# Causal clearing moved from GpSimd to VectorE, and longer lots of probability sums, in an attention-plus-experts kernel on one core

## The chip, the cores and the metric

The kernel runs on one core of a Trainium2 chip. The metric is the device time in microseconds (us) of the whole program. The kernel before took 1740.67 us, the median of 3 runs (1737.72 to 1743.27).

## The reference

What is computed, cut down (x is 2 x 2048 x 512, 16 heads of 32):

```
xn = layernorm(x)
q, k, v = split(xn @ W_qkv)                        # 16 heads of 32
a = q @ k.T / sqrt(32) + alibi + causal_mask       # 2048 x 2048 per head
y = softmax(a) @ v @ W_o
e = argmax(softmax(xn @ wg));  f = gate * (xn @ W[e].T + b[e])   # top-1 of 8 experts
out = x + y + f
```

## The kernel before

The program has four stages: projection and routing, attention (`attend`), the experts, and the sum of the parts. The change touches `attend`, and one line of set-up in the first stage.

**Tiling.** `attend` handles 8 groups of 4 heads (`G`, `HG`). Scores are held transposed, keys on the 128 partitions and queries along the row. A group has 40 rounds (`ROUNDS`): for query chunk c = 0 to 3 (512 queries each) the key blocks 0 to 4c+3 of 128 keys. Chunk 0 is rounds 0 to 3, chunk 1 rounds 4 to 11, chunk 2 rounds 12 to 23, chunk 3 rounds 24 to 39. The last four rounds of each chunk cross the diagonal (`DIAG_OF`, 16 in a group); there only the columns from `off` on are computed, and the 128 x 128 square at `off` has an upper triangle that must be zero.

**A round.** TensorE makes 4 score tiles (L1208, into 3 PSUM banks in turn), ScalarE takes their exponential into `probs` (L1136; 4 slots, so that round r reuses the slot of round r - 4), and later TensorE multiplies the values by it (L1252, `y_ps`). The sums of the softmax (`den_ps`) come from a product with ones. For diagonal rounds it is made from `probs` itself (L1243). The other rounds are first added up on GpSimd in lots (`QUAD_ROUNDS`): `add_quad` makes 4 additions of 128 x 512 for the first two rounds of a lot (L985) and 4 for each further round (L992), and TensorE makes one product for the whole lot (`quad_product`, L1215), two rounds after its last round. Two `quad_sum` buffers are used in turn.

**Waits around the lots.** ScalarE may not write round r before GpSimd has added round r - 4 (`added`, `added_by`): the first two rounds of a lot are released together by its first 4 additions, each further round by its own 4.

**Clearing.** On GpSimd, `clear` zeroes the triangle in all 4 heads of a diagonal round with one instruction (L1001), which signals `cleared`; TensorE waits for it before it uses that round. GpSimd's queue is in order of `SUMMED_OR_CLEARED`: each lot at its last round, each clear at its round, and four multiplications a group (`normalise`, L975).

**VectorE** computes ahead the maximum of each row of scores: TensorE makes `max_ps` tiles (L1176, 3 banks in turn, so that it makes the fourth only when VectorE has taken the first), and VectorE takes the maximum (L1038, and L1034 on the diagonal). A group needs 160 such units. `PLAN_MID` spreads them at 4 a round, rounds 14 on for the next group. In the last group only rounds 0 to 13 have any. VectorE also turns and inverts the sums of a finished chunk (`invert`, L1073, L1077, L1081), for chunk c at rounds 2, 3 and 4 after its last; these come after the maxima of their round.

**TensorE's order** is written out: it visits rounds in pairs. A visit to rounds r, r+1 has 8 score tiles with 8 maxima tiles between them (`visit`); after it come the row sums and value products of the pair before (r-2, r-1). Pairs are called by their rounds below.

**DMA.** The next group's `q_aug` and `k_aug` are loaded when the previous group has ended, and are needed at round 14.

## Time and profile before

| | |
|---|---|
| median of 3 runs | 1740.67 us |
| the profiled execution, whole time | 1743.71 us |
| its span in the profile | 1741.2 us |
| TensorE busy | 1627.1 us, 93% |
| VectorE busy | 1044.1 us, 60% |
| ScalarE busy | 749.0 us, 43% |
| GpSimd busy | 873.1 us, 50% |
| mean granted TensorE clock | 0.965 of full speed |

PE is TensorE, PEld its weight loads, DVE is VectorE, ACT ScalarE, POOL GpSimd. The span is that of the one profiled execution. Attention fills the stretch from 355 to 1470 us of it; its eight groups begin near 368, 550, 680, 812, 946, 1078, 1209 and 1341 us. A line in the timeline merges equal instructions that follow one another: start, time that they take together, engine, source line, operation, tiles, count, and in brackets the idle time of the engine before them with what ended it.

### The profile page before, as it was taken

What the parts mean: (1) busy time and instruction counts of PE and PEld (TensorE: products, weight loads), DVE (VectorE), ACT (ScalarE), POOL (GpSimd) and SP (SyncE); (2) the same over time, 40 slices, a digit from 0 to 9 for tenths busy, and PEclk for the clock granted to TensorE, in tenths of its full rate; (3) what the DMA queues carried; (4) which work ended last, traced back from release to release, by engine and by line L of the source; (5) the groups of instructions that cost most, each with busy time, mean ns of one, the idle gap of its engine ahead of it and who ended that gap; (6) DMA issues with size and microseconds to landing.
All of it is one profiled execution on the core that took longest, in us unless ns stands there. A gap on an engine that the chain in (4) does not pass through costs nothing. (4 is left out here: it accounts for less than half of the span.)

```text
span 1741.2 us, 26967 instructions
## 1 busy us (share of the span) xinstructions
PE 1627.1 (93%) x9266; PEld 991.7 (57%) x9267; DVE 1044.1 (60%) x2451; ACT 749.0 (43%) x1574; POOL 873.1 (50%) x869
## 2 busy tenths in 40 slices
PE   5999999589699999999999999999999997799898
PEld 4888888444344554545554554554545433588686
DVE  6443333488477776867776777777777601544466
ACT  3222222024354654655564655655555564411110
POOL 5500000017685874874875775775775775222350
PEclk9999999769899999999999999999999998899999
DMA  6655654685803603703702702802801401445695
GB/s 239 222 190 181 215 189 168 152 119 104 119 8 75 124 9 79 125 8 73 132 8 61 143 8 51 153 8 49 156 8 60 154 7 59 136 157 164 205 396 213
DMA packets 99244, 205.68 MB, mean 118 GB/s; under 512 B 11164, under 2 KB 28604, under 8 KB 93484
## 3 DMA queue, kind: packets, MB, share of 16 engines
q1 hardware_dynamic: 85208, 172.26, 39.0%
q0 software_dynamic: 9248, 23.53, 4.3%
q10 hardware_dynamic: 4672, 8.41, 1.7%
q8 instruction: 66, 1.08, 0.3%
q14 instruction: 50, 0.41, 0.1%
HBM read 124.55 MB, written 79.07 MB: 117 GB/s over the span
## 5 line engine op out<-in xcount | busy, mean ns | idle before, releaser
L1136 ACT ACTIVATE probs_sb<-score_ps 128x512 f32<-128x512 f32 (+3 forms) x1280 | 585.3, 552 | 475.3 <-PE score_ps L1208 454.9
L1038 DVE TENSOR_REDUCE part_max<-max_ps 128x1 f32<-128x512 f32 x768 | 473.0, 678 | 213.4 <-PE max_ps L1176 213.2
L1176 PE MATMUL max_ps<-k_aug,q_aug 104*128 104x512 f32 (+3 forms) x1280 | 509.2, 410 | 52.2 <-DMA k_aug<-steps_d 34.6
L1208 PE MATMUL score_ps<-q_aug,k_aug 106*128 106x512 f32 (+4 forms) x1280 | 480.1, 398 | 9.6 <-ACT probs_sb L1136 7.4
L985 POOL TENSOR_TENSOR quad_sum<-probs_sb 128x512 f32<-128x512 f32 x288 | 359.9, 1283 | 167.4 <-ACT probs_sb L1136 143.8
L1176 PEld LDWEIGHTS max_ps<-k_aug,q_aug 104*128 104x128 f32 x1280 | 247.7, 194 | 238.1 <-DVE part_max L1038 86.6
L1208 PEld LDWEIGHTS score_ps<-q_aug,k_aug 106*128 106x128 f32 (+1 forms) x1280 | 241.9, 190 | 145.8 <-ACT probs_sb L1136 122.5
L1252 PE MATMUL acc_ps<-probs_sb,v_sb 128*32 128x512 f32 (+3 forms) x2560 | 291.8, 542 | 0.0
L1034 DVE CUSTOM_DVE_ANT_0 max_ps<-max_ps,mask_row 128x384 f32<-128x384 f32 (+3 forms) x512 | 239.1, 513 | 68.9 <-PE max_ps L1176 67.8
L992 POOL TENSOR_TENSOR quad_sum<-quad_sum,probs_sb 128x512 f32<-128x512 f32 x192 | 239.2, 1284 | 0.1
L1001 POOL TENSOR_SCALAR_AFFINE_SELECT probs_sb<-probs_sb 128x512 f32<-128x512 f32 x128 | 80.3, 636 | 205.2 <-ACT probs_sb L1136 204.6
L1252 PEld LDWEIGHTS acc_ps<-probs_sb,v_sb 128*32 128x32 f32 x2560 | 73.5, 111 | 122.7 <-issue 89.6
L959 POOL IOTA token<- 128x32 int32 x1 | 0.2, 154 | 246.7 <-POOLq L393 246.7
L680 DVE SCALAR_TENSOR_TENSOR st_lo<-group_ps,st_hi 128x512 fp32r<-128x512 f32 x64 | 44.2, 691 | 127.2 <-ACT st_hi L732 127.2
L796 PE MATMUL group_ps<-xT_hi,w_hi 128*128 128x512 f32 x256 | 102.3, 399 | 0.0
L796 PE MATMUL group_ps<-xT_hi,w_lo 128*128 128x512 f32 x256 | 101.0, 395 | 0.0
L796 PE MATMUL group_ps<-xT_lo,w_hi 128*128 128x512 f32 x256 | 101.0, 394 | 0.0
L1243 PE MATMUL acc_ps<-probs_sb,ones 128*32 128x512 f32 (+3 forms) x1024 | 96.8, 450 | 0.0
L732 ACT ACTIVATE st_hi<-group_ps 128x512 fp32r<-128x512 f32 x64 | 38.3, 598 | 135.4 <-PE group_ps L796 135.4
L1353 POOL DMA_INDIRECT rows<-xn_d,slot_token x39 | 37.3, 958 | 99.5 <-PE turn_ps L1450 92.1
L1215 PE MATMUL acc_ps<-quad_sum,ones 128*32 128x512 f32 x576 | 75.8, 598 | 0.0
L1073 DVE STREAM_TRANSPOSE acc_sb<-acc_ps 128x512 f32<-128x512 f32 x32 | 22.9, 715 | 86.3 <-PE acc_ps L1252 84.9
(177 smaller groups left out, 1754.0 us busy)
## 6 DMA issues: line engine op xcount, KB each, us to landing
k_aug<-k_hi_d SPq DMA_DIRECT2D x14, 1024.0 KB
q_aug<-q_hi_d SPq DMA_DIRECT2D x14, 1024.0 KB
slot_y_d<-y_rows SPq DMA_DIRECT2D x39, 256.0 KB, 2.0
xn_d<-xn SPq DMA_DIRECT2D x8, 1024.0 KB, 5.5
q_hi_d<-st_hi SPq DMA_DIRECT2D x32, 256.0 KB, 3.5
q_lo_d<-st_lo SPq DMA_DIRECT2D x32, 256.0 KB, 3.6
k_hi_d<-st_hi SPq DMA_DIRECT2D x32, 256.0 KB, 2.5
k_lo_d<-st_lo SPq DMA_DIRECT2D x32, 256.0 KB, 2.8
```

What stands on the lines that cost most here:

```text
L796: last = nc.tensor.matmul(group_ps[:, n % BANKS], lhs, rhs, start=(k == 0 and p == 0), stop=(k == KC - 1 and p == 2))
L985: nc.gpsimd.tensor_tensor(quad_sum[:, t % 2, hh], probs[:, r0 % P_SLOTS, hh], probs[:, r1 % P_SLOTS, hh], ALU.add).then_inc(added, 1)
L992: nc.gpsimd.tensor_tensor(quad_sum[:, t % 2, hh], quad_sum[:, t % 2, hh], probs[:, r % P_SLOTS, hh], ALU.add).then_inc(added, 1)
L1001: nc.gpsimd.affine_select(out=square, in_=square, compare_op=ALU.is_ge, fill=0.0, base=0, pattern=[[0, HG], [1, P]], channel_multiplier=-1 ...
L1034: nc.vector.tensor_tensor_reduce(max_ps[:, bank, 0:w], max_ps[:, bank, 0:w], m.mask_row[:, CH - w:CH], 1.0, LOWEST, ALU.add, ALU.max, part ...
L1038: nc.vector.tensor_reduce(part_max[:, hh * QT + i, kc:kc + 1], max_ps[:, bank, 0:w], AX.X, ALU.max).then_inc(max_taken, 1)
L1136: nc.scalar.activation(probs[:, r % P_SLOTS, hh, off:CH], score_ps[:, (r * HG + hh) % S_BANKS, off:CH], ACT.Exp).then_inc(exp_done, 1)
L1176: nc.tensor.matmul(max_ps[:, bank, 0:w], q_aug[0:ROW_MAX, half, hh, i * P:(i + 1) * P], k_aug[0:ROW_MAX, half, hh, kc * CH:kc * CH + w], s ...
L1208: nc.tensor.matmul(score_ps[:, u % S_BANKS, off:CH], k_aug[rows, half, hh, jb * P:(jb + 1) * P], q_aug[rows, half, hh, cc * CH + off:(cc + ...
L1215: last = nc.tensor.matmul(den_ps[hh * DH:(hh + 1) * DH, :], m.ones[:], quad_sum[:, t % 2, hh], start=start, stop=False)
L1243: nc.tensor.matmul(den_ps[hh * DH:(hh + 1) * DH, off:CH], m.ones[:], probs[:, r % P_SLOTS, hh, off:CH], start=r == FIRST_SUM[cc], stop=r = ...
L1252: last = nc.tensor.matmul(y_ps[hh * DH:(hh + 1) * DH, off:CH], v_sb[:, half, jb, hh * DH:(hh + 1) * DH], probs[:, r % P_SLOTS, hh, off:CH] ...
```

## The change

Four things change.

1. The lots of chunk 2 become 4 and 4 rounds (4, 2, 2 before), those of chunk 3 become 4, 4, 2 and 2 (4, 2, 2, 2, 2 before). A group has 7 lots (9 before). GpSimd's additions go from 60 to 68 a group.
2. GpSimd no longer clears.
3. VectorE clears: after the maxima of the second round of a diagonal pair it waits for the exponentials of each round of the pair and takes the minimum of the square (128 x 512 over 4 heads, in place) and `keep`. In its queue this stands before `invert`.
4. A tile `keep` (128 x 128, bf16) of limits is made by GpSimd at the very start: 3e38 where the probability stays, 0 where it is to be cleared.

```diff
-LOT_SIZES = {1: (4,), 2: (4, 2, 2), 3: (4, 2, 2, 2, 2)}
+LOT_SIZES = {1: (4,), 2: (4, 4), 3: (4, 4, 2, 2)}
...
+        m.keep = sb("keep", [P, P], BF16)
...
-                for t in (m.ident, m.mask_row):
-                    nc.gpsimd.memset(t[:], 0.0).then_inc(blank, 1)
-                pool.wait_ge(blank, 2)
+                for t, fill in ((m.ident, 0.0), (m.mask_row, 0.0), (m.keep, -LOWEST)):
+                    nc.gpsimd.memset(t[:], fill).then_inc(blank, 1)
+                pool.wait_ge(blank, 3)
+                nc.gpsimd.affine_select(out=m.keep[:], in_=m.keep[:], compare_op=ALU.is_ge, fill=0.0, base=0,
+                                        pattern=[[1, P]], channel_multiplier=-1)
...
-                def clear(r, exps):
-
-                    cc, jb = ROUNDS[r]
-                    off = (jb - TPC * cc) * P
-                    square = probs[:, r % P_SLOTS, :, off:off + P]
-                    pool.wait_ge(exp_done, exps + (r + 1) * HG)
-                    nc.gpsimd.affine_select(out=square, in_=square, compare_op=ALU.is_ge, fill=0.0, base=0,
-                                            pattern=[[0, HG], [1, P]], channel_multiplier=-1).then_inc(cleared, 1)
...
-                        if r in DIAG_OF:
-                            clear(r, exps)
-                        else:
+                        if r not in DIAG_OF:
                             add_quad(QUAD_OF[r], first, exps, used, adds)
...
+                def clear(g, r):
+
+                    cc, jb = ROUNDS[r]
+                    off = (jb - TPC * cc) * P
+                    square = probs[:, r % P_SLOTS, :, off:off + P]
+                    dve.wait_ge(exp_done, g * NSU + (r + 1) * HG)
+                    nc.vector.tensor_tensor(square, square, m.keep[:].unsqueeze(1).to_broadcast([P, HG, P]),
+                                            ALU.min).then_inc(cleared, 1)
...
                     for r in range(NR):
                         maxima(events[r], banks, g, units)
+                        if r % 2 and r in DIAG_OF:
+                            clear(g, r - 1)
+                            clear(g, r)
                         if r in INVERT_AT:
```

## Rows read from the trace of the kernel before

**Rows 1.** Third and last group: length, busy of each engine, PEclk, DMA share, GB/s

```profile
680.00:812.00 132.00, 130.43 (x844) 66.83 (x844) 95.95 (x244) 74.86 (x168) 89.56 (x80) 0.99 0.37 70
1341.00:1468.00 127.00, 119.56 (x749) 52.01 (x737) 38.30 (x87) 74.01 (x166) 89.28 (x80) 0.97 0.21 75
```

**Rows 2.** Groups of instructions by form: busy, mean ns | idle before, releaser

```profile
L985 POOL TENSOR_TENSOR quad_sum<-probs_sb 128x512 f32<-128x512 f32 x210 | 262.6, 1284 | 126.3 <-ACT probs_sb L1136 107.0 <-PE acc_ps L1215 19.3
L1001 POOL TENSOR_SCALAR_AFFINE_SELECT probs_sb<-probs_sb 128x512 f32<-128x512 f32 x93 | 58.3, 636 | 116.3 <-ACT probs_sb L1136 115.9
L1551 DVE TENSOR_TENSOR yT_lo<-yT,yT_hi 128x2048 fp32r<-128x2048 f32 x8 | 18.2, 2290 | 21.0 <-ACT yT_hi L1545 21.0
L627 DVE TENSOR_TENSOR more_than<-run,full_f 128x256 f32<-128x256 f32 x1 | 0.4, 427 | 0.0
```

**Rows 3.** Timeline of TensorE, chunk 2 of the third group

```profile
753.35 1.06 PE L1243 MATMUL acc_ps<-probs_sb,ones 128*32 128x512 f32 x8
...
755.10 1.04 PE L1215 MATMUL acc_ps<-quad_sum,ones 128*32 128x512 f32 x8
755.95 0.83 PE L1243 MATMUL acc_ps<-probs_sb,ones 128*32 128x384 f32 x8
```

**Rows 4.** Timelines of VectorE and TensorE, chunk 0 of the fourth group

```profile
816.34 0.71 DVE L1073 STREAM_TRANSPOSE acc_sb<-acc_ps 128x512 f32<-128x512 f32 x1
816.97 2.45 DVE L1038 TENSOR_REDUCE part_max<-max_ps 128x1 f32<-128x512 f32 x4
...
820.18 0.50 PE L1176 MATMUL max_ps<-k_aug,q_aug 104*128 104x512 f32 x1
820.61 1.06 PE L1243 MATMUL acc_ps<-probs_sb,ones 128*32 128x512 f32 x8
```

**Rows 5.** Timeline of VectorE, pairs that follow (8, 9) and (20, 21)

```profile
749.91 2.48 DVE L1038 TENSOR_REDUCE part_max<-max_ps 128x1 f32<-128x512 f32 x4 [2.54 <-PE max_ps L1176]
...
841.83 4.87 DVE L1038 TENSOR_REDUCE part_max<-max_ps 128x1 f32<-128x512 f32 x8 [1.27 <-PE max_ps L1176]
```

**Rows 6.** Timeline of GpSimd, additions of chunks 2, 3 and 1

```profile
738.43 9.94 POOL L985 TENSOR_TENSOR quad_sum<-probs_sb 128x512 f32<-128x512 f32 x8
...
777.04 9.99 POOL L985 TENSOR_TENSOR quad_sum<-probs_sb 128x512 f32<-128x512 f32 x8
...
832.27 9.98 POOL L992 TENSOR_TENSOR quad_sum<-quad_sum,probs_sb 128x512 f32<-128x512 f32 x8
```

**Rows 7.** Timeline of ScalarE: exponentials of pairs (22, 23), (34, 35), (36, 37), (0, 1)

```profile
750.11 1.51 ACT L1136 ACTIVATE probs_sb<-score_ps 128x256 f32<-128x256 f32 x5 [2.85 <-PE score_ps L1208]
...
789.76 4.03 ACT L1136 ACTIVATE probs_sb<-score_ps 128x512 f32<-128x512 f32 x8 [2.76 <-PE score_ps L1208]
796.62 3.60 ACT L1136 ACTIVATE probs_sb<-score_ps 128x512 f32<-128x512 f32 x8 [2.83 <-PE score_ps L1208]
...
813.07 3.60 ACT L1136 ACTIVATE probs_sb<-score_ps 128x512 f32<-128x512 f32 x8 [6.13 <-PE score_ps L1208]
```

**Rows 8.** The last group: additions, and exponentials of pairs (22, 23) and (36, 37)

```profile
1397.91 5.01 POOL L985 TENSOR_TENSOR quad_sum<-probs_sb 128x512 f32<-128x512 f32 x4
1435.62 9.90 POOL L985 TENSOR_TENSOR quad_sum<-probs_sb 128x512 f32<-128x512 f32 x8
1410.49 2.13 ACT L1136 ACTIVATE probs_sb<-score_ps 128x256 f32<-128x256 f32 x8 [2.49 <-PE score_ps L1208]
1454.51 3.60 ACT L1136 ACTIVATE probs_sb<-score_ps 128x512 f32<-128x512 f32 x8 [2.34 <-POOL quad_sum L985]
```

**Rows 9.** TensorE's waits for the next group's load; VectorE in the first group

```profile
PE max_ps L1176 <- DMA q_aug<-q_rows_d: 3.1, 3, 1.5
468.55 0.30 DVE L1034 CUSTOM_DVE_ANT_0 max_ps<-max_ps,mask_row 128x128 f32<-128x128 f32 x1 [14.34 <-PE max_ps L1176]
```

**Rows 10.** Start of two groups, third and fourth: the granted clock (PEclk)

```profile
689.00:693.00 4.00, 4.00 (x32) 0.94 (x24) 1.28 (x3) 0.00 (x0) 1.27 (x1) 0.71 1.02 203
820.00:824.00 4.00, 3.85 (x35) 1.37 (x35) 2.53 (x5) 0.28 (x1) 1.91 (x2) 1.00 1.04 207
```

## Prediction

> **What bounds the kernel now.** First the busy time by stretch. In a middle group of 132 us TensorE is busy for 130.4, VectorE for 96.0, GpSimd for 89.6 [rows 1]: TensorE's written order sets the pace, and what lengthens or shortens one of its steps moves the end. But a matmul that waits for its data counts as near-full too, so I read the timelines to see who releases the next step. Three helpers come close. VectorE paces the maxima tiles: in the last visit of chunk 0 TensorE makes its eighth maxima tile at 820.18, when VectorE has just taken the fifth (it takes one each 0.61, from 816.97, with a short reciprocal after four), and only then starts the row sums at 820.61 [rows 4]. GpSimd paces the reuse of `probs`: additions follow one another every 1.24 to 1.25 us (9.94 / 8) [rows 6]. And the next group's load ends last in three of the middle groups, 3.1 us in all [rows 9]. Group totals hide all three, so the sum has to be made place by place.
>
> **What is saved.** A lot's product holds TensorE from 755.10 to the next product at 755.95, 0.85 us [rows 3]. Two lots fewer in a group, one after visit (20, 21) and one after visit (32, 33), are 1.7 us a group, 13.6 in eight. GpSimd loses 16 clears of 0.636 a group (10.2 us) and gains 8 additions of 1.284 (10.3 us) [rows 2]: its total stays, but the additions come in the two chunks where they are dense and the clears went from places where it idled.
>
> **What a clear costs on VectorE.** No row shows this minimum. The two rows with both inputs in SBUF take 427 ns for 256 columns and 2290 for 2048 [rows 2]: 1.04 ns a column, so 0.69 us for 512 columns, and a pair of clears holds the engine for 1.3 (queued instructions overlap by some 0.07, as the maxima do: 4.87 / 8 = 0.61 [rows 5]). Beside an addition of GpSimd its price is unknown: the rows show none of VectorE's two-input instructions there. Below, it is 0.69 as alone; above, the two take turns, and each clear may wait for a whole addition of 1.28 and hold up the next by 0.65. I take turns as the likelier. GpSimd's addition with two inputs takes twice its select with one (1.284, 0.636 [rows 2]), so fetching the inputs is what it spends its time on, and an engine's second input is just what is new here on VectorE. That is thin evidence, so both sums are given.
>
> The Trainium skill says it outright (SBUF — State Buffer, "Who interferes with whom"): VectorE and GpSimd share a pair of ports as an exclusive lock, and a VectorE instruction with two SBUF inputs contends with a GpSimd instruction that reads SBUF. No row here shows it; by it the upper sum holds, without it the lower.
>
> **Chunk 0, pair (0, 1).** The clears wait for the exponentials, done at 813.07 + 3.60 = 816.67 [rows 7]. Queued behind them are the transpose of the sums, begun at 816.34, and the maxima of the next visit, begun at 816.97 [rows 4]. New first take: 816.67 + 1.3 + 0.63 = 818.6, 1.6 us late. There is no idle time to hide it: visits (0, 1) and (2, 3) follow each other with no products between, and by rows 4 the row sums start with VectorE's fifth take. **+1.6.** The clears of (2, 3) fall in the products after it, and GpSimd is idle at both.
>
> **Chunk 1, pair (8, 9).** VectorE idles 1.27 before 841.83 [rows 5], so it is free at 840.56, and 1.3 just fits: **0** alone. But GpSimd adds until 832.27 + 9.98 = 842.25 [rows 6], with a boundary at 841.0. In turns the first clear runs from 841.0 to 841.7, the second straight after it or after the last addition, and the first take comes at 842.4 or 843.7, 0.6 or 1.8 late: **+1.2**. TensorE's maxima pass it on.
>
> **Chunk 2.** Before, the additions of 16 to 19 ran as eight from 738.43 [rows 6]. Now they are twelve: 738.43 + 12 x 1.245 = 753.4. The exponential of round 23 may not begin before that. It began at 750.11 + 4 x 0.31 = 751.35 [rows 7] and could now begin at 750.5 with the product gone. TensorE's last score tile of the visit needs that exponential's bank, so it follows at 753.7, a maxima tile after it, and the row sums start at 754.4 instead of 753.35 [rows 3]: **+1.05**, the saved 0.85 already counted. In turns, the clears of (20, 21), asked for at 749.91 - 2.54 = 747.4 [rows 5], fall among these additions and push the twelfth to 754.7: **+2.35**. The clears of (22, 23) are hidden in the products that follow.
>
> **Chunk 3.** Here the first twelve additions are as before; from 777.04 come twelve (eight before) [rows 6], done at 792.0. The exponential of round 35 began at 789.76 + 4 x 0.5 = 791.8 [rows 7]: +0.2, again with the 0.85 eaten. The next four additions end at 797.0, and round 36, begun at 796.62 [rows 7], waits for them: **+0.4**, with turns at (36, 37) **+0.6**.
>
> **Middle groups:** alone 1.6 + 0 + 1.05 + 0.4 = 3.05, in turns 1.6 + 1.2 + 2.35 + 0.6 = 5.75. Six of them: 18.3 or 34.5. The load waits swallow up to 3.1 of it [rows 9], since the load begins with the group and is needed at round 14: 15.2 or 31.4.
>
> **Last group.** No maxima after round 13, VectorE almost idle (38.3 us [rows 1]), but the rounds are faster, so GpSimd is closer to the bound. 1.6 and 0 or 1.2 as above; chunk 2: 1397.91 + 12 x 1.245 = 1412.85, in turns 1414.15, against 1410.49 + 1.3 = 1411.8 for round 23: +1.05 or +2.35; chunk 3: 1435.62 + 16 x 1.245 = 1455.5 against 1454.51 for round 36 [rows 8]: +1.0, with turns 1.1. Together 3.65 or 6.25.
>
> **First group.** Chunk 2 ends in a 14.3 us wait for the next load [rows 9], which hides it. Left are +1.6 in chunk 0, 0 or 1.2 in chunk 1, and -0.85 in chunk 3, where its rounds are slower: 0.75 or 2. The tile `keep` costs GpSimd some half microsecond at the start, behind the first loads: 0.
>
> **Sum:** alone 15.2 + 3.65 + 0.75 = +19.6; in turns 31.4 + 6.25 + 2 = +39.6. On the profiled execution's 1743.7 (1741.2 span and 2.5 around it) that is 1763.3 and 1783.3. It lay 3.0 above the median of 1740.7, so in terms of the median 1760 and **1780**. I forecast 1780.
>
> **Rivals.** (a) *Clears run free beside additions:* the alone sum, 1760. For it: nothing in the rows shows turns. Against: the argument above. (b) *Everything is hidden, the products go:* 1740.7 - 13.6 = 1727. It needs the twelve additions of chunk 2 to end by 750.5 instead of 753.4, and a free 1.3 us on VectorE at 816.7. It decides from a pitch of addition below (750.5 - 738.43) / 12 = 1.0 us, which no row shows, unless ScalarE's wait is looser than I read it. Half of the gain, with losses of the same size, would be no change. (c) *The clock drops more often:* at the end of chunk 0 the third group ran at a mean of 0.71 for 4 us where the fourth ran at 1.00 [rows 10], so partly at 1.2 GHz and not 2.4, and the fifth did as the third, just after the visit whose TensorE work was stretched by VectorE. Those two groups lost about 1.6 us there. With that visit stretched further, it may come in all eight: six more times some 1.4 is +8, 1788.
>
> **How the numbers follow.** In turns 0.50, rival (a) and what lies between 0.28, (c) 0.10, (b) 0.08, no change 0.04. The range is 1752 to 1797: below, the alone sum with half of its chunk 0 cost hidden; above, (c) with second clears that always wait. Within 0.3% (5 us) is what a measurement can't tell from no change. Faster 0.08, same 0.04, slower 0.88.
>
> **What would show it.** VectorE's first take after (0, 1) some 2 us behind the last exponential; ScalarE's idle time before round 23 put down to GpSimd's additions; additions in an unbroken row of twelve; in turns, gaps or longer records of both engines around 841 and 748; 448 products L1215 instead of 576; the group's period grown from 132 to about 138 us (135 alone). Wrong would be: a VectorE minimum much shorter than 0.69, additions that run faster in long rows, or a group's period below 131.

## The result, and the profile after

The changed kernel takes **1831.12 us** (median of 4 runs, 1825.09 to 1831.95), the kernel before on the same chip 1739.20 (4 runs, 1736.08 to 1743.27): a ratio of 1.052, 95% interval 1.050 to 1.055. The forecast was 1780 in a range of 1752 to 1797. The sign was right; the loss is 92 us where 39 were forecast.

The groups of instructions of the changed kernel first, by line and form (busy, mean ns of one, idle before).

```profile
L1082 DVE TENSOR_TENSOR probs_sb<-probs_sb,keep 128x512 f32<-128x512 f32 x128 | 146.8, 1186 | 55.7 <-ACT probs_sb L1140 55.7
L995 POOL TENSOR_TENSOR quad_sum<-quad_sum,probs_sb 128x512 f32<-128x512 f32 x320 | 398.4, 1285 | 0.0
L1219 PE MATMUL acc_ps<-quad_sum,ones 128*32 128x512 f32 x448 | 61.8, 626 | 0.0
```

L1219 is the lots' product (576 before, now 448: the change does that part). GpSimd's additions have kept their 1.28. The clear, L1082, has a mean of 1.19. Asked for by its line, it shows what a mean hides:

```profile
L1082 DVE TENSOR_TENSOR probs_sb<-probs_sb,keep x128: 668/682/7154, 377.5 to 1552.5; 128x512 f32<-128x512 f32 x128
```

The median is 0.68, just what was worked out for it (0.69), and the longest 7.15 (in the last group, where VectorE had been idle before it). In the first group no pair takes over 1.4; from the second on some wait, and in the middle groups it is the same three in each. The timeline of VectorE and GpSimd in the third group at these pairs, (8, 9), (20, 21) and (36, 37):

```profile
724.87 4.20 DVE L1082 TENSOR_TENSOR probs_sb<-probs_sb,keep 128x512 f32<-128x512 f32 x2
...
719.20 7.49 POOL L995 TENSOR_TENSOR quad_sum<-quad_sum,probs_sb 128x512 f32<-128x512 f32 x6
726.64 1.28 POOL L978 TENSOR_TENSOR acc_sb<-acc_sb 128x512 f32<-128x512 f32 x1
...
766.17 7.12 DVE L1082 TENSOR_TENSOR probs_sb<-probs_sb,keep 128x512 f32<-128x512 f32 x2
...
762.24 9.90 POOL L995 TENSOR_TENSOR quad_sum<-quad_sum,probs_sb 128x512 f32<-128x512 f32 x8
...
826.01 1.46 DVE L1082 TENSOR_TENSOR probs_sb<-probs_sb,keep 128x512 f32<-128x512 f32 x2
```

Read the ends. The additions of chunk 2 end at 762.24 + 9.90 = 772.14, and the two clears at 773.29, 1.15 later: the first was asked for 0.2 into an addition (762.24 + 3 x 1.24 = 765.96) and has waited for the rest of it and for four more. At (8, 9) GpSimd is done at 727.92 (additions and a multiplication, back to back), and the pair at 729.07, again 1.15 later. At (36, 37) little was left to wait for: that run ended 0.3 after the pair asked. So VectorE did not take turns with GpSimd: it waited for the end of the unbroken run, and GpSimd wasn't slowed at all (8 additions in 9.90, as [rows 6]). Before, VectorE had 2.54 of idle time after (20, 21) and 1.27 after (8, 9) [rows 5]; 7.12 and 4.20 don't fit in. TensorE, and the windows around it, in the same place:

```profile
773.95 0.79 PE L1180 MATMUL max_ps<-k_aug,q_aug 104*128 104x512 f32 x1 [4.92 <-DVE part_max L1030]
```

```profile
769.00:771.00 2.00, 0.02 (x1) 0.00 (x0) 2.00 (x1) 0.48 (x2) 2.00 (x3) 1.00 0.01 4
771.00:773.00 2.00, 0.00 (x0) 0.00 (x0) 2.00 (x2) 0.00 (x0) 1.14 (x1) 0.74 0.00 0
773.00:777.00 4.00, 3.05 (x13) 2.44 (x17) 4.00 (x10) 1.11 (x4) 0.00 (x0) 0.50 0.01 4
```

(The columns are those of [rows 1].) TensorE stands still for 4.92 because VectorE, which holds its three maxima banks, stands in the clear. Then it pays a second time: from 773 to 777 the granted clock is 0.50, that is 1.2 GHz and not 2.4. The forecast expected something else here, a wait of ScalarE for the additions before round 23. In the middle groups there is none: those exponentials wait for TensorE, which has stopped for VectorE (timeline of ScalarE, third group). Only in the last group does ScalarE wait there for the additions, 2.32.

```profile
774.97 0.28 ACT L1140 ACTIVATE probs_sb<-score_ps 128x128 f32<-128x128 f32 x1 [5.48 <-PE score_ps L1212]
```

The list of waits says the same of the whole program. Before, the first of these waits wasn't in it, and the longest of the second was 0.8 us:

```profile
PE max_ps L1180 <- DVE part_max L1030: 57.9, 39, 5.0
PEld max_ps L1180 <- DVE part_max L1030: 132.8, 211, 5.2
```

**Where the 88 us of span went.** A chunk's length is the time between ScalarE's copies of a finished chunk out of PSUM (L1115 before, L1119 after), read from ScalarE's timeline. In the fourth group of after the copies give 16.1, 31.2 and 45.0 for chunks 0, 1 and 2 (the copy at 841.24 is that of the third group's last chunk):

```profile
841.24 0.69 ACT L1119 ACTIVATE acc_sb<-acc_ps 128x512 f32<-128x512 f32 x1
857.37 0.60 ACT L1119 ACTIVATE acc_sb<-acc_ps 128x512 f32<-128x512 f32 x1 [0.71 <-PE acc_ps L1256]
888.56 0.60 ACT L1119 ACTIVATE acc_sb<-acc_ps 128x512 f32<-128x512 f32 x1 [0.89 <-PE acc_ps L1256]
933.54 0.60 ACT L1119 ACTIVATE acc_sb<-acc_ps 128x512 f32<-128x512 f32 x1 [0.89 <-PE acc_ps L1256]
```

The table sums these lengths over the second to the eighth group, each less the same of before, in us. The column for the first group runs from its first copy to its fourth, so its chunk 0 isn't in it. All versions of the attention kernel in the next section are in the table. Two things in it aren't the work of the edits. The kernel before waits for the next group's load ahead of round 14 in three groups, which makes its chunk 1 about 3.7 longer in all; a version without these waits shows -3.7 there. And its chunk 0 ran at a lower clock in two groups.

| kernel | chunk 0 | chunk 1 | chunk 2 | chunk 3 | first group | sum |
|---|---|---|---|---|---|---|
| forecast, in turns | +11.2 | +8.4 | +16.5 | +4.7 | +2.0 | +42.8, less 3.1 of load waits |
| after | +18.5 | +28.6 | +37.5 | +4.2 | -0.4 | +88.4 |
| a_lots: the lots alone | +4.8 | -1.7 | +16.9 | +3.1 | -0.2 | +22.9 |
| b_clears: the clears alone | +18.5 | +28.5 | -2.0 | -1.2 | +0.8 | +44.6 |
| c_oneinput | +19.0 | -3.7 | +16.2 | +4.2 | -0.4 | +35.3 |
| d_hand | +19.6 | -1.9 | +30.8 | +4.7 | +1.6 | +54.7 |
| f_zero | +1.7 | -1.2 | +30.9 | +4.7 | +1.7 | +37.7 |
| i_step | +17.3 | +17.7 | +55.4 | +41.3 | +1.5 | +133.2 |
| g_4242 | -1.7 | -1.4 | -1.0 | -3.6 | -0.7 | -8.4 |

### The profile page after: what moved, and what is told of

It is laid out like the page before. It is cut to its first block and busy times, and to the rows that moved or that the text cites. A ratio compares the mean times of both kernels' runs of the same rounds, so it can differ in the third digit from the quotient of the medians.

```text
span 1829.1 us, 26873 instructions
## 1 busy us (share of the span) xinstructions
PE 1653.8 (90%) x9138; PEld 1005.8 (55%) x9139; DVE 1181.6 (65%) x2579; ACT 750.5 (41%) x1574; POOL 872.3 (48%) x807
## 5 line engine op out<-in xcount | busy, mean ns | idle before, releaser
L1180 PE MATMUL max_ps<-k_aug,q_aug 104*128 104x512 f32 (+3 forms) x1280 | 524.7, 427 | 103.4 <-DVE part_max L1030 57.9
L988 POOL TENSOR_TENSOR quad_sum<-probs_sb 128x512 f32<-128x512 f32 x224 | 279.8, 1286 | 311.2 <-ACT probs_sb L1140 311.2
L1180 PEld LDWEIGHTS max_ps<-k_aug,q_aug 104*128 104x128 f32 x1280 | 257.2, 201 | 284.1 <-DVE part_max L1030 132.8
L995 POOL TENSOR_TENSOR quad_sum<-quad_sum,probs_sb 128x512 f32<-128x512 f32 x320 | 398.4, 1285 | 0.0
L1212 PEld LDWEIGHTS score_ps<-q_aug,k_aug 106*128 106x128 f32 (+1 forms) x1280 | 250.6, 197 | 156.7 <-ACT probs_sb L1140 133.7
L1256 PE MATMUL acc_ps<-probs_sb,v_sb 128*32 128x512 f32 (+3 forms) x2560 | 298.2, 558 | 0.0
L1082 DVE TENSOR_TENSOR probs_sb<-probs_sb,keep 128x512 f32<-128x512 f32 x128 | 146.8, 1186 | 55.7 <-ACT probs_sb L1140 55.7
L978 POOL TENSOR_TENSOR acc_sb<-acc_sb 128x512 f32<-128x512 f32 x32 | 41.1, 1284 | 167.4 <-DVE acc_sb L1073 167.3
L1247 PE MATMUL acc_ps<-probs_sb,ones 128*32 128x512 f32 (+3 forms) x1024 | 112.2, 515 | 0.0
L1026 DVE DVE_READ_ACCUMULATOR2_ANT part_max<- 128x1 f32 x512 | 72.2, 141 | 0.0
```

The lines of the kernel that those rows point to most:

```text
L988: nc.gpsimd.tensor_tensor(quad_sum[:, t % 2, hh], probs[:, r0 % P_SLOTS, hh], probs[:, r1 % P_SLOTS, hh], ALU.add).then_inc(added, 1)
L995: nc.gpsimd.tensor_tensor(quad_sum[:, t % 2, hh], quad_sum[:, t % 2, hh], probs[:, r % P_SLOTS, hh], ALU.add).then_inc(added, 1)
L1026: nc.vector.tensor_tensor_reduce(max_ps[:, bank, 0:w], max_ps[:, bank, 0:w], m.mask_row[:, CH - w:CH], 1.0, LOWEST, ALU.add, ALU.max, part ...
L1082: nc.vector.tensor_tensor(square, square, m.keep[:].unsqueeze(1).to_broadcast([P, HG, P]), ALU.min).then_inc(cleared, 1)
L1180: nc.tensor.matmul(max_ps[:, bank, 0:w], q_aug[0:ROW_MAX, half, hh, i * P:(i + 1) * P], k_aug[0:ROW_MAX, half, hh, kc * CH:kc * CH + w], s ...
L1212: nc.tensor.matmul(score_ps[:, u % S_BANKS, off:CH], k_aug[rows, half, hh, jb * P:(jb + 1) * P], q_aug[rows, half, hh, cc * CH + off:(cc + ...
```

## The experiments

The theories: **RUN** (a clear on VectorE waits for the end of GpSimd's unbroken run, that is of additions that follow one another without a gap), **TURNS** (it waits for one addition at most, as forecast), and the granted clock as a second payer. Diffs are against the changed kernel where nothing else is said.

### One half of the change at a time, and the clear without its second input

a_lots has the new lots and the clears of before on GpSimd; b_clears the clears on VectorE and the old lots:

```diff
-LOT_SIZES = {1: (4,), 2: (4, 4), 3: (4, 4, 2, 2)}
+LOT_SIZES = {1: (4,), 2: (4, 2, 2), 3: (4, 2, 2, 2, 2)}
```

c_oneinput keeps every wait and puts an instruction with one SBUF input in the clear's place. It leaves the clearing out (the triangles stay as they are).

```diff
-                    nc.vector.tensor_tensor(square, square, m.keep[:].unsqueeze(1).to_broadcast([P, HG, P]),
-                                            ALU.min).then_inc(cleared, 1)
+                    nc.vector.tensor_reduce(square, square.unsqueeze(3), AX.X, ALU.max).then_inc(cleared, 1)
```

> The longer lots alone, GpSimd still clears. Three theories of the changed kernel's +92 us. RUN: a VectorE instruction with two SBUF inputs waits until GpSimd's unbroken run of instructions ends, however long. TURNS: it waits for the one addition in flight, as the prediction had it. LOTS: the longer lots themselves cost most of it, through ScalarE's wait for the additions. RUN and TURNS expect what the prediction worked out for additions that come late less the saved products: +1.05 and +0.4 in a middle group, some 2 in the last, -0.85 in the first, so about +10, 1749 to 1750 us. LOTS expects 1790 or more.

> The clears on VectorE alone, the old lots. RUN: in chunk 1 the run of 12 additions is the same, so the pair (8, 9) still costs some 3.8 us a group; in chunk 2 the additions end at about the time the clears are asked for, so the 5.6 us there go nearly all; chunk 0 keeps 3.4. Eight times some 7.5 is +55 to +60, 1795 us, and no clear record over some 5 us. TURNS: 1.6 and 1.2 a group and the clock, under +30, 1765. LOTS: within 10 us of before.

> The changed kernel with a VectorE instruction of one SBUF input (a maximum over an axis of length one, in place, 128 x 512) in the place of each minimum; same place, same waits, about the same length. It leaves out the clearing of the triangles. RUN and TURNS: every record is 0.68 us whatever GpSimd does; chunk 1 costs nothing, chunk 2 about 1, chunk 0 keeps 3.4, so about +36 to +40, 1775 us. If the wait has nothing to do with the second input (a queue, the exponentials, the place in the order), the time stays at 1831 and records of 4 and 7 us remain.

Measured, beside 1741.63 of before (7 runs) on the same chip: a_lots **1766.82** (ratio 1.015, 1.011 to 1.018), b_clears **1785.47** (1.025, 1.023 to 1.027), c_oneinput **1778.88** (1.021, 1.019 to 1.023).

c_oneinput by the clear's line:

```profile
L1082 DVE TENSOR_REDUCE probs_sb<-probs_sb x128: 662/679/689, 375.7 to 1498.1; 128x512 f32<-128x512 f32 x128
```

The longest of 128 is 0.689, though it falls beside the same additions. With one input nothing waits: chunk 1 is back at its old length (25.8 us in every group, 30.4 on the mean with the minimum), and 1.3 us of VectorE cost nothing there. So the two-input minimum is what waits, and the whole price of that is 88.4 - 35.3 = 53 us of the 88. The masked maxima of the changed kernel have two inputs as well, but one of them in PSUM (`max_ps`). 362 of the 512 begin beside one of GpSimd's additions, and the longest of those takes 0.737, where one without an addition beside it has taken 0.735 (by the line of the masked maxima, in ns):

```profile
L1026 DVE CUSTOM_DVE_ANT_0 max_ps<-max_ps,mask_row x512: 275/502/737, 342.7 to 1467.9; 128x128 f32<-128x128 f32 x43, 128x384 f32<-128x384 f32 x43, 128x512 f32<-128x512 f32 x43, 128x256 f32<-128x256 f32 x42
```

So it is the second input in SBUF that matters, and not two inputs as such. In chunk 1 the wait delays VectorE by 4.20 - 1.27 = 2.9 a group and TensorE stops for 2.4. That makes 25.8 + 2.9 = 28.7; what the groups take is 29.6 or 31.2, at a lower clock (windows that each hold exactly chunk 1, third and fourth group of after):

```profile
713.79:743.37 29.58, 27.08 (x169) 13.99 (x170) 25.90 (x47) 14.65 (x33) 16.35 (x14) 0.94 0.88 153
857.37:888.56 31.19, 28.70 (x169) 14.38 (x170) 25.90 (x47) 14.63 (x33) 16.35 (x14) 0.89 0.84 147
```

So the wait for the run is behind all of the loss in chunk 1, and 0.9 to 2.5 us of it a group is the clock (an estimate, from these lengths).

b_clears shows the same with the old lots. Its 1785 lies between the 1795 that RUN expected and the 1765 of TURNS; what tells them apart is chunk 1, +28.5, the same as in the changed kernel and more than three times what turns were forecast to cost. Its pair (20, 21) waits too, 2.23 us, to the end of the run (753.64 + 9.94 = 763.58) and 1.16 on:

```profile
762.51 2.23 DVE L1082 TENSOR_TENSOR probs_sb<-probs_sb,keep 128x512 f32<-128x512 f32 x2
...
753.64 9.94 POOL L988 TENSOR_TENSOR quad_sum<-probs_sb 128x512 f32<-128x512 f32 x8
```

That wait costs nothing in chunk 2, since the run ends early enough. In chunk 2 the halves don't add: -2.0 and +16.9 apart, +37.5 together. The missing 22.6 come with the clears of (20, 21), which meet a run with four more additions to come only where the lot is four rounds long (with the old lots only its end, above). The second input alone, after less c_oneinput, is 37.5 - 16.2 = 21.3.

a_lots: the forecast for this half was 1.05 us for chunk 2 of each group; it is 16.9 / 7 = 2.4. ScalarE's wait is where it was forecast, at the exponential of round 23 (fourth group; timeline of ScalarE and GpSimd, and the windows after it):

```profile
887.76 0.62 ACT L1136 ACTIVATE probs_sb<-score_ps 128x128 f32<-128x128 f32 x3 [2.79 <-POOL quad_sum L992]
...
877.75 9.93 POOL L992 TENSOR_TENSOR quad_sum<-quad_sum,probs_sb 128x512 f32<-128x512 f32 x8
```

```profile
886.00:888.00 2.00, 0.44 (x1) 0.19 (x1) 1.53 (x6) 0.24 (x2) 2.00 (x3) 0.80 0.00 0
888.00:894.00 6.00, 5.91 (x26) 1.69 (x30) 0.63 (x2) 0.65 (x4) 2.03 (x4) 0.50 0.00 0
894.00:896.00 2.00, 2.00 (x22) 0.85 (x15) 0.03 (x1) 0.00 (x0) 0.00 (x0) 0.99 0.00 0
```

TensorE idles 1.6 us in 886 to 888, and for the 6 us behind it the clock is at 1.2 GHz. The idle is what the sum counted; the slow stretch is what it left out. c_oneinput shows the two apart, since its stop of 1.6 comes in every middle group but the clock doesn't fall in two of them (windows that each hold exactly chunk 2, fourth and third group):

```profile
869.58:909.04 39.46, 37.55 (x243) 19.59 (x244) 29.50 (x91) 22.55 (x51) 31.03 (x26) 1.00 0.03 11
732.13:774.72 42.59, 40.66 (x243) 20.21 (x244) 29.52 (x91) 22.56 (x51) 31.05 (x26) 0.92 0.03 8
```

Before it was 38.62: +0.84 at full clock, near the forecast 1.05, and 3.1 more at 0.92. (a_lots' third group, 37.90, has no stop at all in chunk 2; it had waited 1.57 for its load just ahead of it.)

### The clock in chunk 0

Chunk 0 has no additions beside it, and the one-input clear costs it as much as the minimum (+19.0, +18.5), so no second input is at work there. Windows that each hold exactly chunk 0: of before, the second and the third group; of after, the second and the third; of c_oneinput, the fourth.

```profile
553.63:566.48 12.85, 12.28 (x96) 6.52 (x95) 10.11 (x25) 6.96 (x19) 5.21 (x6) 1.00 1.03 204
684.23:698.67 14.44, 13.88 (x96) 6.82 (x95) 10.10 (x24) 6.96 (x18) 5.21 (x6) 0.88 1.02 203
```

```profile
554.64:568.69 14.05, 12.50 (x96) 6.51 (x95) 12.52 (x29) 6.96 (x19) 3.33 (x3) 1.00 1.02 202
697.48:713.79 16.31, 15.01 (x96) 7.59 (x95) 12.52 (x28) 6.95 (x19) 3.31 (x3) 0.79 1.02 203
```

```profile
828.46:843.76 15.30, 13.89 (x95) 6.93 (x95) 12.47 (x27) 6.95 (x18) 3.31 (x3) 0.89 1.02 203
```

The same 96 matmuls take 12.85, 14.05, 14.44, 15.30 or 16.31 us. At a clock of 1.00 the clears cost 14.05 - 12.85 = 1.2, the delay of VectorE itself (forecast 1.6). The rest is the clock: 0.88 or 0.89 costs 1.3 to 1.6 (15.30 - 14.05, 14.44 - 12.85), and 0.79 costs 2.3 (16.31 - 14.05). Before, two groups of seven were at 0.88; after, six of seven are at 0.79. Ahead of the fall in the third group stands a stop of TensorE for want of a maxima bank (1.01 us, then the clock row of the next 5 us). The same stop stands in the second group, at 557.05, and there the clock stays at 1.00:

```profile
557.05 0.50 PE L1180 MATMUL max_ps<-k_aug,q_aug 104*128 104x512 f32 x1 [1.01 <-DVE part_max L1030]
699.88 0.50 PE L1180 MATMUL max_ps<-k_aug,q_aug 104*128 104x512 f32 x1 [1.01 <-DVE part_max L1030]
```

```profile
699.00:700.00 1.00, 0.12 (x1) 0.12 (x2) 1.00 (x3) 0.30 (x1) 0.00 (x0) 1.00 0.96 188
700.00:705.00 5.00, 4.99 (x21) 2.63 (x25) 5.00 (x10) 1.11 (x4) 0.00 (x0) 0.53 1.04 206
```

Nor does the fall need this stop. In a_lots, where chunk 0 is as before and GpSimd clears, five of seven groups are at 0.88 (before: two), with no stop of TensorE over 0.32 us there; that is its +4.8. Its fourth group:

```profile
818.62:833.07 14.45, 13.91 (x96) 6.83 (x95) 10.11 (x25) 6.97 (x19) 5.21 (x6) 0.88 1.03 204
```

Counted over all versions, chunk 0 was below full clock in 11 of 28 groups where GpSimd clears it (before, a_lots, f_zero, g_4242), never below 0.88, and in 34 of 35 where VectorE does (after, b_clears, c_oneinput, d_hand, i_step), 21 of them at 0.79 or 0.80. So the clears there make the fall nearly certain and often deeper; what decides in the single group stays open.

This is rival (c) of the prediction, which had a chance of 0.10 and was priced at 1.4 for six groups; here it is paid in chunk 0 and again in chunks 1 and 2.

### GpSimd hands over

If GpSimd stops for the clears at a chosen place, the wait for the run should go. d_hand makes it wait for the pair (8, 9) before the last addition of round 7, and for (20, 21) before the first of round 19. f_zero has this and the clears of chunk 0 back on GpSimd, with a semaphore of their own (`cleared0`).

```diff
+                HANDOVER = {(7, HG - 1): 9, (19, 0): 21}
...
+                            if (r, hh) in HANDOVER:
+                                pool.wait_ge(cleared, clears + (DIAG_OF[HANDOVER[r, hh]] + 1))
```

```diff
+                        if r < TPC:
+                            clear_first(r, exps)
+                        elif r not in DIAG_OF:
...
-                        if r % 2 and r in DIAG_OF:
+                        if r % 2 and r in DIAG_OF and r >= TPC:
```

> The changed kernel with two gaps made in GpSimd's runs: before the last addition of round 7 it waits for the clears of (8, 9), before the first addition of round 19 for those of (20, 21). RUN: VectorE gets in at once; chunk 1 falls from +3.8 to about +1, chunk 2 from +5.6 to about +2.4, six us a group less, 1783 us, although GpSimd now waits more. TURNS: VectorE would have got in anyway, so GpSimd's new waits only cost: 1831 or more.

> The kernel with the two gaps, and the clears of chunk 0 given back to GpSimd, which is idle there; chunks 1 to 3 stay on VectorE. If what chunk 0 lost is VectorE's lateness by two clears and the fall of TensorE's clock behind it, chunk 0 goes back from some 16.3 to 12.9 to 14.5 us a group, about 20 us in all: 1772 to 1778 us. If the clock falls there anyway, only 1.6 a group comes back: 1782.

Measured: d_hand **1795.38** (1.030, 1.028 to 1.032), f_zero **1780.30** (1.023, 1.021 to 1.025; its before 1739.54, 17 runs). The pair (20, 21) now takes 2.22 instead of 7.12, and GpSimd goes on as soon as it is done (d_hand):

```profile
762.19 2.22 DVE L1087 TENSOR_TENSOR probs_sb<-probs_sb,keep 128x512 f32<-128x512 f32 x2
...
758.25 5.01 POOL L999 TENSOR_TENSOR quad_sum<-quad_sum,probs_sb 128x512 f32<-128x512 f32 x4
764.58 2.50 POOL L999 TENSOR_TENSOR quad_sum<-quad_sum,probs_sb 128x512 f32<-128x512 f32 x2 [1.32 <-DVE probs_sb L1087]
```

The run ends at 763.26 and the pair at 764.41, 1.15 behind it: a run made shorter makes the wait shorter by as much, as RUN says and TURNS doesn't. Chunk 1 is back to -1.9 (26.07 a group, where c_oneinput has 25.82). But chunk 2 is still +30.8. The 1.32 in which GpSimd stands is pushed onto the twelfth addition, which was late already (its four after the handover end at 756.80 + 4.95 = 761.75 in f_zero, twelve additions and a stop after 745.54), and the exponential of round 23 waits for it: TensorE stops for 2.6 there, 1.6 in a_lots. So my expectation of d_hand was 12 too low: in chunk 2 the time can be taken from VectorE or from GpSimd, but not from neither. f_zero brings chunk 0 from +19.6 back to +1.7, which is all that it gains on d_hand. Its 1780 lies between the two cases expected; by chunk 0 itself, 12.8 to 14.6 a group, it is the first.

### A gap after each addition

i_step makes GpSimd wait, before each addition, for the end of the one before, so that there is no unbroken run.

```diff
+                        wait_past(pool, added, adds + sum(ADDS_OF[:t]) + hh)
...
-                            pool.wait_ge(added, adds + (added_by(r) - 2 * HG + hh + 1))
+                            pool.wait_ge(added, adds + (added_by(r) - HG + hh))
```

> The changed kernel, where GpSimd waits before each addition for the one before it to end. The run is no longer unbroken: if a short gap of 0.1 us is enough for VectorE, the waits of 4.2 and 7.1 us at (8, 9) and (20, 21) fall to under 2 us, and chunk 1 goes from 30 to 27 us, chunk 2 from 44 to 43 (additions that take 0.1 longer each hold ScalarE a little longer): 1795 to 1805. If a gap of that length lets nobody in, the waits stay and the additions are slower: 1831 to 1845.

Measured: **1874.25** (1.078, 1.075 to 1.080). By its line, and at the pair (20, 21), with additions in a row:

```profile
L1083 DVE TENSOR_TENSOR probs_sb<-probs_sb,keep x128: 668/687/1787, 376.8 to 1596.4; 128x512 f32<-128x512 f32 x128
```

```profile
778.12 3.45 DVE L1083 TENSOR_TENSOR probs_sb<-probs_sb,keep 128x512 f32<-128x512 f32 x2
...
772.41 1.26 POOL L989 TENSOR_TENSOR quad_sum<-probs_sb 128x512 f32<-128x512 f32 x1
773.81 2.68 POOL L996 TENSOR_TENSOR quad_sum<-quad_sum,probs_sb 128x512 f32<-128x512 f32 x2
```

The longest clear is now 1.79 instead of 7.15, and a pair inside a run takes 3.45: that is TURNS. The waits fell as expected, but the time is some 70 us above the 1795 to 1805 expected. A gap of 0.14 after each addition (773.81 - 772.41 - 1.26) is enough to let VectorE in. It is no remedy, since the pitch of an addition grows from 1.24 to some 1.4 (772.41 to 773.81, and the two of 2.68), and the chunks that are bound by additions pay (+55, +41).

### The same pair of instructions by themselves

Seven kernels of our own compute nothing of the reference; they run GpSimd's additions and VectorE's minima of 128 x 512 side by side. Their core, here of k_late, and what the others change in it:

```python
for i in range(RUN):                       # GpSimd: an unbroken run
    ...                                    # (a wait that is long satisfied; the first four add two probs)
    nc.gpsimd.tensor_tensor(quad[:, 0, h], quad[:, 0, h], probs[:, i // 4 % 2, h], ALU.add).then_inc(p_done, 1)
...
dve.wait_ge(p_done, n * RUN + asked)       # VectorE: asks after so many additions
for i in range(2):
    nc.vector.tensor_tensor(square(i), square(i), keep[:].unsqueeze(1).to_broadcast([P, 4, P]), ALU.min)
```

- e_micro: select, fill or waits on GpSimd, one-input maximum or twelve minima on VectorE
- h_micro2: forms of the operands, waits ahead of each addition
- j_micro3: an instruction of 64 to 512 columns ahead, ScalarE as releaser, ScalarE or TensorE beside, x as data
- l_place: as k_late, with `filler = sb("filler", [P, 24 * 1024], F32)` ahead of `probs`
- m_scan: `CASES = [8 * w for w in range(1, 65)]`, columns of the instruction ahead; n_beside: the same with `BESIDE = True`

> A kernel of its own that computes none of the reference: six cases, twice each. Cases 1 to 4: GpSimd has 12 instructions of 128 x 512 in a row; after its third VectorE is released for two of its own. Case 1: additions against two-input minima; 2: additions against one-input maxima; 3: selects (one input) against minima; 4: fills (no input) against minima; 5: as 1, but GpSimd waits for each of its own to end before it starts the next; 6: VectorE has 12 minima in a row and GpSimd is released for two additions after the third. RUN: in 1 the first minimum lasts until the twelfth addition ends, some 11 us; in 3 likewise, some 5; in 2 and 4 0.7; in 5 it gets in after one addition, under 2 us. TURNS: in 1 and 3 no minimum over 2 us. No sharing: 0.7 everywhere. In 6 GpSimd waits for the whole run (RUN both ways) or for one minimum.

> In the first kernel of its own VectorE and GpSimd took turns (a minimum of 1.7 us), in the changed kernel the minimum waited for the whole run. What differs? Seven cases, twice each, none of the reference computed; always 12 additions of GpSimd on tiles shaped as in the kernel, and two minima of VectorE released after the third. 1: flat operands, additions without waits; 2: the kernel's minimum (4 heads x 128 columns out of rows of 512, limits repeated over heads); 3 and 4: as 1 and 2, with satisfied waits ahead of each addition, as in the kernel; 5: flat, limits repeated; 6: 4 x 128 out of 512, limits flat; 7: flat, limits in f32. OPERANDS: 2 and 4 wait for the run's end (10 us), 1 and 3 take turns, and 5 or 6 says which part. WAITS: 3 and 4 wait for the run's end, 1 and 2 take turns. NEITHER: all take turns, and the cause is something that only the whole kernel has.

> In both kernels of its own the engines took turns; in the changed kernel, never. Eleven cases, twice each, none of the reference computed; always 12 additions on GpSimd with satisfied waits, and two minima as in the kernel. What changes is when VectorE asks (a one-input instruction of 64, 192, 320 or 512 columns ahead of the minima, or an instruction of ScalarE that releases it), what runs beside (20 instructions of ScalarE, 20 matmuls), and whose data GpSimd adds (constants, or the input). In the two kernels before, VectorE always asked within 0.2 us of the start of an addition. PHASE: a minimum that asks late in an addition waits for the run's end, 5 to 10 us; an early one takes turns. BESIDE: only the cases with ScalarE or TensorE wait. DATA: only those with the input. None: all take turns.

> A kernel of its own, which computes none of the reference: GpSimd makes unbroken runs of 20 additions of 128 x 512, and VectorE asks for two minima with keep after 1, 3, 6, 8, 10 or 13 of them, in four of the ten cases straight after 4 to 12 maxima from PSUM (the last ones with the mask). In the earlier kernels of this kind it asked after 3, and two minima took 3.3. The theory that the place in the run decides (in the attention kernel the clears came after 5 to 8 additions): 3.3 when asked after 1 or 3, but after 6, 8, 10 and 13 the rest of the run, some 17, 15, 12 and 9. The theory that VectorE's own work ahead decides: 3.3 wherever nothing is ahead, and long waits in the four cases with maxima. The theory that it is neither: 3.3 in all ten.

> The same ten cases with the probabilities and sums 96 KB further up in each partition's SBUF, keep and the mask staying at its start, as they lie in the attention kernel behind its large operands. If the place in SBUF decides how the two engines share it, minima wait for the run here and not in the run beside it; otherwise the two runs agree case by case.

> A kernel of its own, which computes none of the reference: 64 runs of 14 unbroken additions on GpSimd; after the fifth, VectorE takes a maximum of 8, 16, ... 512 columns from PSUM and then asks for two minima, so that the moment of asking moves through half of an addition in steps of some 8 ns. If the moment within the addition decides, a block of neighbouring cases waits for the whole run (a pair some 8 to 10) and the rest take turns (3.3). If it is chance, as the one case of twenty in k_late may be, single long pairs are scattered, some 3 of 64. If something that only the attention kernel has decides, all 64 take 3.3.

> The same 64 cases, with ScalarE taking exponentials from PSUM into SBUF and TensorE multiplying beside every run. If their traffic makes VectorE lose its turn, many or all of the 64 pairs take 8 to 10; if it doesn't, as many as in m_scan.

e_micro, timeline: minima L38, one-input maxima L41; additions L28, selects L31, fills L35 of GpSimd beside them.

```profile
15.06 3.33 DVE L38 TENSOR_TENSOR vec_a<-vec_a,vec_b 128x512 f32<-128x512 f32 x2 [7.19 <-POOL pool_a L28]
30.81 1.28 DVE L41 TENSOR_REDUCE vec_a<-vec_a 128x512 f32<-128x512 f32 x2 [12.42 <-POOL pool_a L28]
...
43.74 2.04 DVE L38 TENSOR_TENSOR vec_a<-vec_a,vec_b 128x512 f32<-128x512 f32 x2 [11.65 <-POOL pool_a L31]
...
51.51 1.29 DVE L38 TENSOR_TENSOR vec_a<-vec_a,vec_b 128x512 f32<-128x512 f32 x2 [5.73 <-POOL pool_b L35]
```

Two minima take 3.33 beside additions, 2.04 beside selects and 1.29 beside GpSimd's fills, which read nothing; two instructions with one input take 1.28 beside additions. So GpSimd must read for a dispute, and of VectorE's two instructions only the one with two inputs is in it. But here the engines take turns: the wait is one addition, not the run. The same holds where GpSimd waits for its own last addition (3.42 for two minima) and the other way round: two additions asked for in a run of twelve minima take 3.22, where two have taken 2.5.

That held in all seven cases of h_micro2 (operands shaped as in the kernel, waits already satisfied ahead of each addition; 3.30 for two), in all eleven of j_micro3 (2.6 to 3.34; the moment of asking, 0.14 to 0.87 into an addition, ScalarE as releaser, ScalarE and TensorE beside, real data), in the 20 pairs of l_place, in the 64 of m_scan and in the 64 of n_beside: none of m_scan's 128 minima is over 1.75.

```profile
L70 DVE TENSOR_TENSOR probs<-probs,keep x128: 1028/1659/1747, 20.3 to 1164.9; 128x512 f32<-128x512 f32 x128
```

In k_late 19 of 20 pairs took turns, and one did what the attention kernel does. Its two repetitions of one case (asked for after 13 of 20 additions), each with GpSimd's run:

```profile
146.81 20.45 POOL L46 TENSOR_TENSOR quad<-quad,probs 128x512 f32<-128x512 f32 x16
157.96 3.30 DVE L72 TENSOR_TENSOR probs<-probs,keep 128x512 f32<-128x512 f32 x2 [25.83 <-POOL quad L46]
...
401.58 19.56 POOL L46 TENSOR_TENSOR quad<-quad,probs 128x512 f32<-128x512 f32 x16
412.73 9.56 DVE L72 TENSOR_TENSOR probs<-probs,keep 128x512 f32<-128x512 f32 x2 [25.84 <-POOL quad L46]
```

Both ask 11.15 us into the run. The first pair takes 3.30 and stretches the run by 0.89; the second takes 9.56, to 1.15 us past the end of the run (421.14), and the run keeps its length. So the long wait also comes without the attention kernel's code, and the same code can give either. The theory that the place in the run decides fell (turns after 1 to 13 additions), and so did the maxima ahead, the place in SBUF, the moment within the addition (up to 0.87 into it; the attention kernel's longest waits began 0.2 into one), and the two other engines. What makes the long wait the rule in the attention kernel and one in some 200 pairs here stays open.

### A longer lot where nothing waits

The product saved is worth something if the longer lot stands where nothing waits for its additions. g_4242 is the kernel before with one line changed: the last twelve rounds of chunk 3 in lots of 2, 4 and 2, and nothing else.

```diff
-LOT_SIZES = {1: (4,), 2: (4, 2, 2), 3: (4, 2, 2, 2, 2)}
+LOT_SIZES = {1: (4,), 2: (4, 2, 2), 3: (4, 2, 4, 2)}
```

> The kernel before, all clears on GpSimd, with one product fewer: chunk 3 in lots of 4, 2, 4, 2 and chunk 2 as it was. By the same walk as in the prediction the additions of rounds 30 to 33 end at 797 on the third group's time, before the exponential of round 37 needs them, so nothing waits and 0.85 us a group is saved, in seven or eight groups: -6 us, 1735. If the longer lots are bad in themselves, it is slower than before.

Measured: **1734.11** (12 runs, 1729.70 to 1738.45) against 1739.54 (17 runs): ratio 0.997, 0.996 to 0.998. In the middle groups chunk 3 went from 53.4 to 52.5, the 0.85 of one product; the last group, which has faster rounds, lost 1.5 there (47.88, before 46.33). It is a gain of 0.3%: small, with an interval that lies below 1. The -8.4 of its profile in the table holds more than the edit, -1.7 of it one chunk 0 fewer at the lower clock.

## Why the prediction failed, by its own steps

- **Right: the direction, the places, and the price of an undisturbed clear.** VectorE's median is 0.68 (0.69 forecast). Chunk 1 without a dispute costs 0, as "1.3 just fits" said (c_oneinput, 25.8 in every group; its -3.7 are load waits of before). Chunk 3 measured +0.3 to +0.4 in the middle groups (+0.6 forecast), and the product is 0.85 (g_4242). ScalarE's wait before round 23 is put down to GpSimd's additions in a_lots and c_oneinput; in the changed kernel only in the last group, since in the others the longer stop for the clears has taken its place.
- **The step that failed: "the two take turns, and each clear may wait for a whole addition of 1.28."** What the runs show in its place is a wait for all that is left of the unbroken run: 4.20 for (8, 9), and 7.1 for (20, 21). In chunk 1 that is +28.6 instead of +8.4, the lower clock behind each stop included. In chunk 2 it is 37.5 - 16.9 - (-2.0) = 22.6, where the step gave 1.3 x 7 = 9.1. The direction of it was also wrong: "push the twelfth to 754.7" has the additions yield, and they didn't (8 in 9.90). The step bounded the wait by one addition with no row that said so; its upper end should have been the run, which [rows 6] show at 10 us.
- **Mis-sized: chunk 2 without the dispute.** "+1.05" measured 2.4 (a_lots). The difference is the granted clock, which fell to 1.2 GHz for some 6 us after the stop; at full clock it is +0.84 (c_oneinput).
- **Mis-sized: chunk 0.** "+1.6" is 1.2 at full clock, and 2.6 on the mean of seven groups, the rest again by the clock. Rival (c) named this mechanism and its price was near; it was taken for an alternative to the main case and for chunk 0 alone. The runs show it together with the main case and in chunks 1 and 2 too, so it belonged in the sum as a term of its own.
- **What was hidden:** the first group's sum, forecast at +2.0, was -0.4. Of the forecast, +1.6 was for its chunk 0, which the column leaves out and which cost nothing: from ScalarE's first exponential to that first copy it is 23.6 us, and was 23.7. In the rest no clear met a long run, and chunk 2's loss went into the wait for the load.
- **The rivals:** (a), clears that run free, would be c_oneinput: 1778.88, not the 1760 worked out for it; the difference is the clock in chunks 0 and 2. (b) and no change had no part in it. The range ended at 1797, since its upper case combined second clears that always wait with (c) in chunk 0 alone.

The sum: 88.4 - 39.6 = 48.8 us more than forecast. The wait for the run, with the clock behind it, has 28.6 - 8.4 = 20.2 of it in chunk 1 and 22.6 - 9.1 = 13.5 in chunk 2, the clock behind the lots' stop in chunk 2 16.9 - 7 x 1.05 = 9.6, and chunk 0 has 7.3. From these 50.6 go 2.0 (chunk 2 of b_clears), 0.5 (chunk 3) and 2.4 (first group), and 3.1 come back that the forecast took off for load waits and that the measured lengths contain.

The Trainium skill (SBUF — State Buffer, "Who interferes with whom") says that a VectorE instruction with two inputs in SBUF contends with a GpSimd instruction that reads SBUF, and that one with a single input, or a GpSimd instruction that only writes, doesn't contend; e_micro and c_oneinput agree in all three (3.33, 1.28 and 1.29 for two). Under "SBUF: two separate sides" the same page calls the pair of ports an exclusive lock, held for the whole instruction. The turns of e_micro agree with that; the 7.15 of the changed kernel and the 8.95 of k_late go beyond it.

## What to carry to other kernels

Before an instruction moves to VectorE, count its inputs in SBUF: with two, its price beside GpSimd's additions can be the rest of their unbroken run, not its own length and not one instruction, so that is the upper end to reckon with. Where TensorE can be made to stop for 1 to 5 us, add the slower clock that may stand behind the stop (in this kernel 1.3 to 2.3 us in a chunk 0 and up to 3.1 in a chunk 2). And where two edits meet in one stretch, as the longer lots and the clears did, work out their sum with both in place: apart they cost 23 and 45, together 88.

## What the runs showed of the hardware

- Of two repetitions of the same code, one took turns and one waited for the whole run: 3.30 and 9.56 for the same two minima (k_late).
- A break of 0.14 us between additions is enough for turns: longest clear 1.79 instead of 7.15 (i_step).
- In turns both engines lose: the minimum takes 1.65 to 1.75 instead of 0.68, and the run grows by 0.89 for a pair (20.45 against 19.56 for 16 additions, k_late).
- Chunk 0's 96 matmuls took from 12.85 to 16.31 us with the granted clock at 1.00 down to 0.79. A stop of TensorE of 1 us stood ahead of it in six groups of the changed kernel, but the same stop in the second group was followed by no fall, and five groups of a_lots fell to 0.88 with no stop over 0.32 us.
